# A pipelined grouped-query attention: the residual add ahead of the row maximum, one exponential ahead of the key norms, and the layer norm's last operation on GpSimd

## The reference

```python
x = x + _L1_xattn_ref(_layernorm(x, axis=-1), ctx_2048, Wq, Wk, Wv, Wo, ...)

q = (draft_hidden @ Wq.T).reshape(bsz, draft_len, H, HD)      # H = 16 heads of 128
q = _rms_norm(q, q_norm_w).transpose(0, 2, 1, 3)
kv_in = jnp.concatenate([context_hidden, draft_hidden], axis=1)   # 128 + 128 keys
k = (kv_in @ Wk.T).reshape(bsz, total_len, KVH, HD)           # KVH = 4 groups
v = (kv_in @ Wv.T).reshape(bsz, total_len, KVH, HD).transpose(0, 2, 1, 3)
k = _rms_norm(k, k_norm_w).transpose(0, 2, 1, 3)
q = _rope(q, draft_position_ids);  k = _rope(k, full_position_ids)
scores = jnp.einsum('bhqd,bhkd->bhqk', q, k) * SCALE
probs = jax.nn.softmax(scores, axis=-1)
attn = jnp.einsum('bhqk,bhkd->bhqd', probs, v)
return attn.transpose(0, 2, 1, 3).reshape(bsz, draft_len, H * HD) @ Wo.T
```

## Time and profile before

| | |
|---|---|
| time, median of 3 runs | 916.38 us |
| the runs | 924.61, 916.38, 912.51 us |
| the profiled execution: its time, and its span | 912.91 us, 911.2 us |
| busy in the span | PE 698.8 us (77%), DVE 731.0 us (80%), ACT 656.7 us (72%), POOL 463.5 us (51%) |
| of these in 305 to 840 us, the second attention | PE 446.75, DVE 437.58, ACT 429.70, POOL 351.88 us |
| granted TensorE clock in 305 to 840 us | 0.96 |

### The profile page before, as it was taken

One profiled execution on the slowest core, in us unless ns is written; L12 is line 12 of the kernel. 1 busy time (PEld: TensorE's weight loads), 2 busy tenths in 40 slices (PEclk: granted clock), 3 DMA queues, 4 the chain that ended last, 5 costly groups with the idle time before them and its releaser, 6 DMA issues. The chain is left out here.

```text
span 911.2 us, 16830 instructions
## 1 busy us (share of the span) xinstructions
PE 698.8 (77%) x4627; PEld 425.1 (47%) x4627; DVE 731.0 (80%) x1826; ACT 656.7 (72%) x2172; POOL 463.5 (51%) x637
## 2 busy tenths in 40 slices
PE   0194988988366567988898889888988988876776
PEld 0161333333133245665566556555655655643343
DVE  7676688984699378988898889789887978875996
ACT  1665778774399169988798889779887978962542
POOL 1500011122366387767677767667666767621453
PEclk9995899998799799999999999899998999998997
DMA  8303445543045237976676668666776666761245
GB/s 294 124 1 110 128 139 162 158 131 92 20 82 104 41 73 132 145 129 126 115 134 124 120 126 136 103 117 122 134 122 128 116 110 124 133 105 32 45 102 124
DMA packets 321999, 103.91 MB, mean 114 GB/s; under 512 B 286932, under 2 KB 321142, under 8 KB 321654
## 3 DMA queue, kind: packets, MB, share of 16 engines
q1 hardware_dynamic: 321910, 102.89, 54.3%
HBM read 22.10 MB, written 6.29 MB: 31 GB/s over the span
## 5 line engine op out<-in xcount | busy, mean ns | idle before, releaser
L1353 ACT ACTIVATE psum<-psum,arena 128x256 f32<-128x256 f32 x256 | 136.3, 532 | 7.8 <-DVE arena L1401 7.8
L1253 POOL TENSOR_TENSOR arena<-arena 128x512 f32<-128x512 f32 x64 | 81.1, 1268 | 114.4 <-DVE arena L1381 114.3
L1496 PE MATMUL psum<-wo_t,arena 128*128 128x256 f16 x768 | 102.2, 287 | 43.5 <-DVE x_rows L1421 43.4
L1381 DVE TENSOR_TENSOR arena<-psum,arena 128x1024 f32<-128x1024 f32 x64 | 78.4, 1225 | 52.1 <-PE psum L1452 52.1
L1309 ACT ACTIVATE arena<-psum,arena 128x256 f16<-128x256 f32 x256 | 100.3, 474 | 18.0 <-issue 16.3
L1496 PEld LDWEIGHTS psum<-wo_t,arena 128*128 128x128 f16 x768 | 77.6, 102 | 72.7 <-issue 50.5
L1362 DVE SCALAR_TENSOR_TENSOR arena<-psum,arena 128x256 f16<-128x256 f32 x256 | 110.7, 474 | 0.5 <-ACT arena L1309 0.5
L1452 PE MATMUL psum<-wq_t,arena 128*128 128x512 f16 x384 | 98.5, 395 | 13.3 <-DMA arena<-arena 6.7
L1320 ACT ACTIVATE arena<-psum 128x128 f32<-128x128 f32 x256 | 68.0, 299 | 55.2 <-DVE arena L1381 55.2
L1484 PE MATMUL psum<-arena 128*128 128x512 f16 x384 | 94.5, 382 | 15.1 <-DVE arena L1389 14.5
L1474 PE MATMUL psum<-arena 128*128 128x256 f16 x768 | 94.3, 273 | 2.9 <-DMA arena<-arena 1.9
(11 more groups left out here) (189 smaller groups left out, 1679.4 us busy)
## 6 DMA issues: line engine op xcount, KB each, us to landing
arena<-split_scratch SPq DMA_DIRECT2D x96, 64.0 KB, 2.7
arena<-arena SPq DMA_TRANSPOSE x272, 3.2
arena<-in_x SPq DMA_DIRECT2D x32, 128.0 KB, 2.2
split_scratch<-arena SPq DMA_DIRECT2D x32, 128.0 KB, 1.8
arena<-in_L_ffn_w SPq DMA_DIRECT2D x2, 1024.0 KB, 6.8
x_rows<-in_L_xattn_Wq SPq DMA_DIRECT2D x1, 2048.0 KB, 13.6
ctx_t<-in_L_xattn_Wo SPq DMA_DIRECT2D x1, 2048.0 KB, 11.7
arena<-in_ctx SPq DMA_DIRECT2D x16, 128.0 KB, 2.2
```

The costliest lines, as they stand in the source:

```text
L1253: eng.tensor_tensor(straight(q_rot[:, :, :]), straight(q_cs[:, 0, :, :]), swapped(q_cs[:, 1, :, :]), ALU.add).then_inc(S["q_rot"], 1)
L1353: last = eng.activation(s_banks(u)[:, h, :], s_banks(u)[:, h, :], ACT.Exp, bias=bias[:, u % 2, h:h + 1], scale=r_q(u)[:, h:h + 1], accum_o ...
L1381: eng.tensor_tensor(q_cs[:, :, :, :], Q_BANK.rearrange("p (h d) -> p h d", h=SHARE).unsqueeze(1).broadcast_to([P, 2, SHARE, HEAD_DIM]), tu ...
L1496: mm = eng.matmul(O_BANK, a_t[:, u % 2, a, P * h:P * h + P], c.wo_t[:, w, SHARE * g + h, :], start=(g == 0 and h == 0 and n == 0), stop=(g ...
```

## The change

Three things move, and nothing is computed otherwise.

1. The residual add of a batch (L1421 before, L1408 after) stands ahead of the row maximum instead of near the end of DVE's step. `lows(u, 1)` moves from behind `v_lo` to ahead of the keys.
2. On ACT the high half of the values stands ahead of the logarithm, and the exponential that makes `r` stands between the first and the second of the four score exponentials.
3. `y` is made on POOL in the HALVES step, one step later than DVE made it.

```diff
 def pool(eng):
             b = batch(s, HALVES)
             if b is not None:
+                eng.wait_ge(S["rstd"], 2 * (b + 1))
+                eng.tensor_scalar(y[:, :], c.x_rows[:, b, :], mv[:, 0:1], rstd[:, :], ALU.subtract, ALU.mult)\
+                   .then_inc(S["y"], 1)
                 eng.wait_ge(S["y"], b + 1)
 def scalar(eng):
+                wait(eng, S["attn"], u - 7)
+                eng.activation(v[:, u % 8, 0, :, :], kv_view[:, :, 1, :], ACT.Copy).then_inc(S["v_hi"], 1)
                 eng.wait_ge(S["ss_q"], u + 1)
                 eng.wait_ge(S["ss_k"], u + 1)
                 wait(eng, S["r"], 2 * u)
                 eng.activation(log_ms[:, :], sums[:, u % 2, :], ACT.Ln, scale=1.0 / HEAD_DIM, bias=eps[:, 1:2])\
                    .then_inc(S["r"], 1)
-                wait(eng, S["attn"], u - 7)
-                eng.activation(v[:, u % 8, 0, :, :], kv_view[:, :, 1, :], ACT.Copy).then_inc(S["v_hi"], 1)
-                eng.wait_ge(S["r"], 2 * u + 1)
-                wait(eng, S["bias"], u - 7)
-                wait(eng, S["k_cs"], u - 7)
-                eng.activation(r[:, u % 8, :], log_ms[:, :], ACT.Exp, scale=-0.5).then_inc(S["r"], 1)
...
+            score = unit(s, SCORE)
+            if score is not None:
+                eng.wait_ge(S["bias"], score + 1)
+                wait(eng, S["share"], 2 * (score - 1))
+                exponential(score, 0)
+            u = unit(s, PROJ)
             if u is not None:
...
+                eng.wait_ge(S["r"], 2 * u + 1)
+                wait(eng, S["bias"], u - 7)
+                wait(eng, S["k_cs"], u - 7)
+                eng.activation(r[:, u % 8, :], log_ms[:, :], ACT.Exp, scale=-0.5).then_inc(S["r"], 1)
+            if score is not None:
+                for h in range(1, SHARE):
+                    exponential(score, h)
 def vector(eng):
             if probs is not None:
                 lows(probs, 0)
+            b = batch(s, LAST)
+            if b is not None:
+                eng.wait_ge(S["o"], GROUPS * (b + 1))
+                eng.scalar_tensor_tensor(c.x_rows[:, b, :], O_BANK, 1.0 / (W_SCALE * W_SCALE * P_SCALE * A_SCALE),
+                                         c.x_rows[:, b, :], ALU.mult, ALU.add).then_inc(S["out"], 1)
             if score is not None:
...
+            if probs is not None:
+                lows(probs, 1)
             if proj is not None:
...
-            if probs is not None:
-                lows(probs, 1)
-            b = batch(s, LAST)
-            if b is not None:
-                eng.wait_ge(S["o"], GROUPS * (b + 1))
-                eng.scalar_tensor_tensor(c.x_rows[:, b, :], O_BANK, 1.0 / (W_SCALE * W_SCALE * P_SCALE * A_SCALE),
-                                         c.x_rows[:, b, :], ALU.mult, ALU.add).then_inc(S["out"], 1)
...
-            b = batch(s, ROWS)
-            if b is not None:
-                eng.wait_ge(S["rstd"], 2 * (b + 1))
-                wait(eng, S["y_lo"], b)
-                eng.tensor_scalar(y[:, :], c.x_rows[:, b, :], mv[:, 0:1], rstd[:, :], ALU.subtract, ALU.mult)\
-                   .then_inc(S["y"], 1)
```

More of the change, by code:

```diff
@@ L1296, in scalar, with exponential @@
         eng.wait_ge(S["eps"], 2)
+        def exponential(u, h):
+            last = eng.activation(s_banks(u)[:, h, :], s_banks(u)[:, h, :], ACT.Exp, bias=bias[:, u % 2, h:h + 1],
+                                  scale=r_q(u)[:, h:h + 1], accum_out=total[:, u % 2, h:h + 1])
+            if h == SHARE - 1:
+                last.then_inc(S["exps"], 1)
         for s in range(STEPS):
@@ L1347, in scalar @@
                 eng.activation(rstd[:, :], log_var[:, :], ACT.Exp, scale=-0.5).then_inc(S["rstd"], 1)
-            u = unit(s, SCORE)
-            if u is not None:
[L1350 to L1356, removed]
+            score = unit(s, SCORE)
[4 more added lines that the diff above has]
+            u = unit(s, PROJ)
+            if u is not None:
+                eng.wait_ge(S["r"], 2 * u + 1)
[5 more added lines that the diff above has]
+                    exponential(score, h)
     def vector(eng):
```

## The result

The changed kernel takes 871.79 us (median of 4 runs, 869.53 to 883.27) against 917.48 us in the same comparison: a ratio of 0.9488, 95% interval 0.9407 to 0.957. The profiled execution took 869.53 us with a span of 867.8, against 912.91 and 911.2. I had forecast 866, and 866.4 for this execution. Now and then an execution is a per cent or so longer at a lower granted clock, and ratios leave it out (here the one of 883.27).

What follows compares the result with a forecast made beforehand. It took a DVE-ACT loop every step and a residual-add wait every batch as the bound. Steps of 6.77, 6.80, 6.77 and 7.53 us make 27.87 a batch, 369.3 against 415.8: 912.9 − 46.5 = 866 us, range 852 to 888.

Steps and rivals of the forecast that it cites:

- `r`: On ACT, its exponential moves between the first two score exponentials and adds 0.10 us to a step, bounds 0 and 0.20.
- the rows step: The step where DVE made `y`: without it, it loses 0.55 us and takes 6.77 us.
- the residual step: The step with the residual add, where POOL now makes `y`: 6.77 + 0.36 + 0.4 of collisions, 7.53 us.
- The knot: Once a batch PE idles 3.09 us for DVE's residual add, delaying DVE 2.42 us; moving the add, costing 0.36, removes it.
- The low halves: On DVE, `lows(u, 1)` ahead of the keys makes keys and `v_lo` about 0.86 us later, at cost 0.
- the ring: Maximum, exponentials, sums, q product and low halves form a loop over DVE and ACT: 6.67 us in a plain step.
- The statistics step: The step with statistics on DVE, beside the exponentials: they now cost almost nothing, 6.80 us instead of 7.19.
- `y` on POOL: `y` takes 0.6 us there, bounds 0.48 and 0.72; collisions with small DVE operations cost 0.4, bounds 0 to 0.8.
- second loop: From maximum through `v_lo` and PE's L1463 to the end of the scores: 6.3 us, with 0.4 us to spare.
- Only the residual moves pay: Rival, chance 0.08: DVE's other steps keep 6.67, 7.19 and 7.22 us; 28.11 a batch, 870 us.
- Every step collides: Rival, chance 0.13: small DVE operations stop behind POOL by 0.4 us in all four steps; 29.07 a batch, 882 us.
- the fourth: Rival, chance 0.02: denser PE work lowers its clock, steps take 13.0 us; slower if 20% of steps do.

Runs made afterwards that it cites:

- `y` alone: The kernel before the change with only `y` moved to POOL in the HALVES step: 920.91 us, ratio 1.0003.
- `y` on DVE with `r` first: The changed kernel with `y` back on DVE and the exponential for `r` ahead of all four score exponentials: 855.86 us, ratio 0.9313.
- the tables moved: The changed kernel with POOL's table work of the residual step moved to the step with nothing by batch: 868.26 us, ratio 0.944.
- a memset of the same 1.22 us: The changed kernel with `y` back on DVE and a memset of an unused tile at its old place on POOL: 872.78 us, ratio 0.9477.

## Why the prediction was right, step by step

One edit at a time, the stretch of 53 steps went: before 415.8, the add moved 369.7, the low halves moved 361.3, ACT's two moves 363.2, `y` to POOL 372.7. So the 43.1 us are −46.1, −8.4, +1.9 and +9.5. My terms for the same four were −43.3 (9.37 to 7.03 us, 13.25 times, and the 12.3 us of low clock), 0, −1.2 (+5.3 for `r`, −6.5 for the room that it gives the statistics) and −2.0 (0.55 off the rows step, 0.4 of collisions on the residual step): 46.5 in all. The add carries the total and was right. The other three I had as a gain of 3.2 us, and they were a loss of 3.0: a gain of 8.4 that I had at nothing, and a cost of 9.5 that I had as a small gain. That these two cancel but for 1.1 us is luck, and the total is close for that reason too.

- **The knot: right, mechanism and size.** The residual step of the kernel with the add alone is 6.96 against 7.03 by my terms, and PE's clock no longer fell. The add's 0.36 us is there almost in full (6.96 − 6.62).
- **The low halves: costed at 0, worth 8.4 us.** I had read that keys and `v_lo` come later and that nothing on the ring waits for them. That holds. What I left out is that later keys shift POOL's work against `part`, and that keys had waited for `r`. I had used the collision only as a risk; it was already being paid in the statistics and the rows step, and the timeline had it:

```profile
528.35 0.55 DVE L1372 TENSOR_SCALAR arena<-arena 128x4 f32<-128x4 f32 x1
...
535.69 0.42 DVE L1372 TENSOR_SCALAR arena<-arena 128x4 f32<-128x4 f32 x1 [0.17 <-ACT psum L1353]
```

- **The statistics step: 6.80 said, 6.71 measured, for a wrong reason.** I had the ring's 0.10 us for `r` make room for the statistics. With the low halves moved and no such room the step is already 6.61, as short as a plain one. Of its 0.52 us before, 0.38 were the 0.55 us of `part` above, a collision that I had taken for the length of the statistics. The 0.10 of `r` then only lengthens it.
- **The rows step: 6.77 said, 6.78 measured, for a wrong reason.** I gave it to `y` leaving DVE. With `y` alone moved it stays 7.21, and with `y` back on DVE it is 6.87. `y` is worth 0.09 us there. The low halves bring 0.25; the kernel with all ACT moves and `y` on DVE has another 0.09.
- **`r`: 0.10 said, 0.10 measured,** on ACT (514.27 to 514.37) and in the plain and statistics steps when it is undone. But I had charged it to all four steps, 5.3 us, and it cost 2.0 (361.2 to 363.2, from `y` on DVE with `r` first to `y` on DVE): in the rows step `r` first costs as much by the collision. The values ahead of the logarithm cost and brought nothing, as I had said (361.3 to 361.2, from the add and the low halves to `y` on DVE with `r` first).
- **`y` on POOL: the mis-sized term, and with it the sign.** I took 0.6 us from the nearest rows; it took 1.22 in all 16 batches. The Trainium skill's ratio (GPSIMD Engine Reference, "Elementwise — side-by-side cycle accounting") had given 1.1 as an estimate, and its rule to use DVE for elementwise work agrees with the 9.5 us. The residual step came out at 7.54 against my 7.53, but POOL was then late into the next one, where `bias` took 0.54: 7.08 instead of 6.77. That step's 0.31 us, less 0.09 in the statistics step, is the difference between 27.87 and 28.11 us a batch, and so nearly all of the 3.4 us by which the stretch missed.
- **A sign I read wrongly beforehand:** PE waiting for `v_lo` was to mean that the second loop is too long. It waited 36 times and set nothing.
- **Rivals.** "Only the residual moves pay" gave the same batch, 28.11, and is nearest in time, but not in cause: the other moves cancel. "Every step collides" came true in two steps of four. Of the fourth there is no sign: the clock was 0.99.

Not settled: why `bias` is released 0.56 us after `y` starts and not at its end; and which of `y`'s differences from POOL's 0.48 us operation (float32 out, two scalars from memory) makes it 1.22.

## What to carry to other kernels

When two engines form a ring, look first for the once-a-batch operation that stands last on one engine and that another must wait for: moving it to where its input has just come cost 0.36 us a batch and gave 3.5 net. Read the durations of the smallest operations on the ring: one that takes 0.5 us in some steps and 0.17 in others, and ends with a GpSimd operation, is being stopped by it, and the remedy here was to shift either of the two or to take work off GpSimd, not to shorten the ring (with `r` first 0.1 us was gained in two steps and lost again in a third). And don't relieve an engine whose operation lies beside the ring by giving it to GpSimd: take it off alone first, and see whether the step moves at all. Do this where the knot is already gone: beside it the cost of `y` did not show, without it it was 9.5 us.

## What the hardware showed that was not expected

- `part` (a `tensor_scalar` of 4 columns, SBUF to SBUF) waits for the POOL operation that is running, low half of q or rotation, high or low half of the keys, and ends 0.02 us behind it: 0.36, 0.43, 0.46, 0.56, 0.67 and (`y` alone) 1.08 us instead of 0.17. If the POOL operation has 0.15 us or less to go, `part` takes its 0.14 to 0.17: it gets into the gap of 0.07 us ahead of the next one. It also took 0.16 where it started 0.01 us into the high half of the keys (rows step with `y` on DVE).
- `bias`, with two SBUF inputs, was stopped by POOL's table product (0.54 and 0.53 us) and by the first 0.56 us of `y`, not by the later part of `y` (with the tables moved it started 0.87 us into `y` and took 0.16) and not by a memset of the same 1.22 us. The Trainium skill (SBUF — State Buffer, "Who interferes with whom") has the second input contend only with a GpSimd instruction that reads SBUF: by that, the memset agrees and the table product too. For the two-port modes it has the pair held for the whole instruction and gives no other length for this case; behind the table product `bias` did wait to the end, inside `y` it was let go at 0.56 of 1.22 us.
- The same operation of 128 x 256 took 0.40 us on DVE at the shortest and 0.52 to 0.71 in most batches, 0.60 to 0.62 on ACT, and 1.22 on POOL.
